# Tokens laid out by time up to the first experts, the recurrence in six chunks of 32 steps

## What is computed

```python
h = concat([patches @ proj_w.T + proj_b + pos_emb,                 # 64 tokens a sample
            segm_table[mask] + sinusoid + token_table[x_txt]])     # 128 tokens a sample
# block 0: a linear recurrence over time in 64 blocks of 3 channels
x = layernorm(h)
b, d, u = x @ W_biv + b_biv, sigmoid(x @ W_decay + b_decay), x @ W_in + b_in
s_t = d_t * rotate(s_{t-1}, axis * angle = b_t) + u_t              # t = 0..191
h = h + s
# block 0: experts, top two of eight, one hidden layer of 288, gelu
h = h + sum_k gate_k * expert_{top k}(layernorm(h))
# block 1: linear attention with 12 heads, then layernorm and experts (768 hidden, silu)
h = h + attention(layernorm(h));  h = h + experts2(layernorm(layernorm(h)))
```

## Time and profile before

| | |
|---|---|
| median of three runs | 540.99 us |
| profiled execution, its own time | 542.78 us |
| its span | 541.0 us |
| VectorE busy | 305.7 us, 57% of the span |
| TensorE busy | 373.5 us, 69% |
| ScalarE busy | 157.5 us, 29% |
| GpSimd busy | 210.9 us, 39% |
| mean clock granted to TensorE | 0.80 of full |

### The profile page before, as it was taken

One profiled execution on the slowest core, in us unless ns is written; L12 is line 12 of the kernel. 1 busy time (PEld: TensorE's weight loads), 2 busy tenths in 40 slices (PEclk: granted clock), 3 DMA queues, 4 the chain that ended last, 5 costly groups with the idle time before them and its releaser, 6 DMA issues.

```text
span 541.0 us, 8003 instructions
## 1 busy us (share of the span) xinstructions
PE 373.5 (69%) x2351; PEld 317.8 (59%) x2351; DVE 305.7 (57%) x1493; ACT 157.5 (29%) x315; POOL 210.9 (39%) x207
## 2 busy tenths in 40 slices
PE   5795002040272699999619989781599999999993
PEld 5442001030162488888508758681499999999992
DVE  4879999999858245445365236969333333333320
ACT  1299405120034011111025111444043333333320
POOL 4204696900002467776300000005445555465433
PEclk9698555555555599999859999765599999999998
DMA  9465000000010112222199900042112333333222
GB/s 250 43 168 121 1 1 1 1 30 1 0 59 1 51 59 81 73 81 76 38 294 312 269 2 0 0 138 67 57 32 50 54 51 52 53 53 53 43 23 22
DMA packets 35884, 37.29 MB, mean 69 GB/s; under 512 B 5898, under 2 KB 32190, under 8 KB 35842
## 3 DMA queue, kind: packets, MB, share of 16 engines
q1 hardware_dynamic: 24342, 21.28, 14.0%
q0 software_dynamic: 9312, 14.00, 12.9%
q10 hardware_dynamic: 2188, 1.49, 1.0%
HBM read 26.41 MB, written 10.35 MB: 68 GB/s over the span
## 4 chain that ended last, share of the span: by engine, by line
PE 34%; DVE 29%; DMA 24%; issue 7%; ACT 3%; POOL 1%; POOLq 1%; SPq 0%; DVEq 0%; ACTq 0%
DMA out<-reg,idxs 20%; DVE bank L992 8%; DVE reg L982 8%; PE bank L1497 7%; PE bank L1456 6%; PE bank L1601 3%; PE bank L1399 3%; PE bank L1483 2%; PE bank L1613 2%; PE bank L1538 2%; DVE st L886 2%; PE bank L1381 1%; DMA con<-in_consts 1%; PE bank L1442 1%; POOL reg L572 1%
## 5 line engine op out<-in xcount | busy, mean ns | idle before, releaser
L1497 PE MATMUL bank<-reg 128*128 (+1 forms) x558 | 105.7, 335 | 1.4 <-DVE reg L1172 0.7
L1497 PEld LDWEIGHTS bank<-reg 128*128 128x128 f32 (+1 forms) x558 | 90.1, 191 | 11.8 <-issue 7.8
L599 POOL DMA_INDIRECT out<-reg,idxs x31 | 49.0, 1582 | 63.3 <-DMA out<-reg,idxs 52.3
L583 POOL DMA_INDIRECT reg<-xn_rows,idxs x62 | 60.5, 977 | 30.2 <-issue 17.9
L1183 DVE TENSOR_SCALAR reg<-bank,gs 128x192 f32<-128x192 f32 x31 | 13.0, 418 | 96.5 <-PE bank L1497 96.5
L992 DVE TENSOR_REDUCE bank<-reg 128x6 f32<-128x24 f32 x384 | 53.3, 184 | 0.0
L982 DVE TENSOR_TENSOR reg<-reg,bank 128x24 f32<-128x24 f32 x384 | 51.7, 175 | 0.1
L1471 PE MATMUL bank<-xTs,xT 128*128 128x128 f32 x372 | 47.9, 280 | 0.0
L1471 PEld LDWEIGHTS bank<-xTs,xT 128*128 128x128 f32 x372 | 45.2, 196 | 0.0
L752 ACT ACTIVATE reg<-bank 128x384 f32<-128x384 f32 x31 | 15.2, 491 | 99.8 <-PE bank L1475 99.8
L1381 PE MATMUL bank<-con,xn 128*96 128x128 f32 x72 | 14.2, 358 | 37.3 <-ACT xn L653 37.3
(11 more groups left out here) (246 smaller groups left out, 756.1 us busy)
## 6 DMA issues: line engine op xcount, KB each, us to landing
reg<-in_w2b SPq DMA_DIRECT2D x8, 576.0 KB, 9.2
reg<-in_w1b SPq DMA_DIRECT2D x8, 384.0 KB, 9.3
reg<-in_w1a SPq DMA_DIRECT2D x8, 216.0 KB
reg<-in_w2a SPq DMA_DIRECT2D x8, 216.0 KB
xn_rows<-xn SPq DMA_DIRECT2D x4, 384.0 KB, 2.6
reg<-in_w1b SPq DMA_DIRECT2D x16, 96.0 KB, 7.9
xn<-expert_rows SPq DMA_DIRECT2D x3, 384.0 KB, 6.6
a<-expert_rows ACTq DMA_DIRECT2D x3, 384.0 KB, 8.0
```

The costliest lines, as they stand in the source:

```text
L583: pool.indirect_dma_start(xs[:, i % RING, 0:(D, D2)[l]], None, xd[l], bass.IndirectOffsetOnAxis(ap=idxs[:, i:i + 1], axis=0)).then_inc(xs_ ...
L599: pool.indirect_dma_start(out, bass.IndirectOffsetOnAxis(ap=idxs[:, i:i + 1], axis=0), ys[:, i % RING, :], None, compute_op=ALU.add).then_ ...
L1497: ins = MM(bank[6][:, 0:D], (hTs if l == 0 else hT2[:, p])[0:r, c * P:(c + 1) * P], w2v[0:r, bass.ds(e * (nhc * D) + c * D, D)], start=(c ...
```

## The change

The host now orders patches and text by time. Tile 2q+f of the first block holds 32 consecutive steps of four samples, with partition = 4 * time + sample; a pair of tiles is one chunk (chunks 0 and 1 are the patches, 2 to 5 the text). TCH is 32, there are six chunks, buffers of the matrix preparation exist twice. For each chunk:

- `bivectors(c)` and `inject(c)` replace `projections`: products with 64 output rows and 128 moving columns, 32 and 24 instructions (24 and 24 for chunk 0, its decay with 8 apart), written directly to the half of the partitions where the scan wants them.
- ScalarE's `front(c)`: sigmoid of the decay, squares directly from PSUM, one copy of the bivectors, one strided copy of the inputs into the matrices.
- `table_of(func)`: a one-column activation that loads the next table in advance.
- The states of chunk g, when ScalarE has copied them, are transposed back with `h` added in PSUM by TensorE (`back(g)`), and ScalarE copies the sum to `h` (`h_copy`). Norm start, norm end, transposes, logits and top two of chunk g lie at fixed step numbers of the next chunks.
- Text embeddings are added by GpSimd; text norms lie inside chunk 0's steps.
- The small constants come in an array `small` of their own, loaded first; `sinpos` and `bp` come in chunk layout (393 and 295 KB) into the region of the first experts' weights.
- The normalized rows are written to `xn_rows` in batch order, four DMAs a chunk, and `h` to `h_rows` likewise; after the last chunk `h` is loaded back in batch order, and the gates go through `gate_rows` and 16 DMAs. `xn_rows` and `expert_rows` have 2048 rows for each of the two choices, part of them padding, and index constants follow.

The diff at its core:

```diff
-TCH = 64
+TCH = 32
@@ matrices: two buffers of each, 128 columns
         def unit(n):
-            v = carve(reg1, n * U)
-            return v.rearrange("p (c a t) -> p c a t", c=n, a=NCH)
+            return [carve(reg1, n * U).rearrange("p (c u) -> p c u", c=n) for _ in range(2)]
@@ SyncE
-            for g in range(3):
-                js = slice(4 * g, 4 * g + 4)
-                sp.wait_ge(xn_ready, NJ + 4 * g + 4)
-                sp.dma_start(tok_rows(xd[0])[:, js, :], xn[:, js, :]).then_inc(xd_written, 16)
+            for g in range(NCHUNK):
+                sp.wait_ge(xn_ready, NJ + 2 * g + 2)
+                to_batch(sp, xd[0], xn, g, xd_written)
+                sp.wait_ge(h_copied, g + 1)
+                to_batch(sp, hd, h, g, h_stored)
+            sp.wait_ge(h_stored, 16 * NCH * NCHUNK)
+            by_batch(sp, h, hd, [h_loaded] * 3)
+            sp.wait_ge(gate0_ready, 1)
+            sp.dma_start(gd, gate[:, :, :].rearrange("p k j -> p (k j)")).then_inc(gate_stored, 16)
...
@@ GpSimd
+            for q in range(4):
+                pool.wait_ge(seg_ev, q + 1)
+                pool.wait_ge(gath[q], 32)
+                nc.gpsimd.tensor_tensor(h[:, js, :], h[:, js, :], xn[:, js, :], ALU.add).then_inc(emb_ready, 1)
...
-            for c in range(1, NCHUNK):
-                prep_angle(pool, nc.gpsimd, link, c)
-                prep_matrix(pool, nc.gpsimd, link, c)
+            # sum_squares, reduce_angle, prep_matrix of 1, the same of 2, then
+            sum_squares(3); reduce_angle(3); sum_squares(4); prep_matrix(3); reduce_angle(4); prep_matrix(4)
+            sum_squares(5); reduce_angle(5); prep_matrix(5)
@@ ScalarE
+            def front(c):
+                xb, yb = proj_banks(c)
...
+                act.wait_ge(proj_mm, 2 * c + 1)
+                if c:
+                    nc.scalar.activation(dec[:, c * U:(c + 1) * U], xb[:, 3 * U:4 * U], ACT.Sigmoid)
+                if c >= 2:
+                    act.wait_ge(th2_ready, c - 1)
+                xv = xb[:, 0:3 * U].rearrange("p (c u) -> p c u", c=3)
+                nc.scalar.activation(sq[c % 2], xv, ACT.Square).then_inc(sq_ready, 1)
+                if c:
+                    nc.scalar.activation(biv[:, :, c * U:(c + 1) * U], xv, ACT.Copy)
+                    injections(c)
+            # from chunk 1 on, every call takes its place in this order (table_of in brackets)
+            front(1) [sqrt] theta(1) [sin] trig(1) [sqrt] ln_std(1,2) ln_std(1,3) ln_norm(1,2)
+            xt_evac(2) ln_norm(1,3) [sigmoid] front(2) [sqrt] theta(2) ln_std(1,4) ln_std(1,5)
+            [sin] xt_evac(3) trig(2) ln_norm(1,4) ln_norm(1,5) keep_states(0) xt_evac(4) xt_evac(5)
+            h_copy(0) [sigmoid] front(3) front(4) [sqrt] theta(3) ln_std(2,0) [sin] trig(3)
+            ln_norm(2,0) [sqrt] theta(4) keep_states(1) xt_evac(6) h_copy(1) [sin] trig(4)
+            [sigmoid] front(5) [sqrt] ln_std(2,1) theta(5) ln_norm(2,1) keep_states(2) xt_evac(7)
+            h_copy(2) [sin] trig(5) [sqrt]
+            for g in range(2, NCHUNK - 1):
+                ln_std(2, g); ln_norm(2, g, h); xt_evac(NPAIR + g); keep_states(g + 1); h_copy(g + 1)
@@ VectorE
+            begin(0); recip_of(1); steps(0, 4); ln_text(2); ln_text(3); steps(4, 6); ln_end(1, 2)
+            ln_end(1, 3); steps(10, 4); ln_text(4); ln_text(5); steps(14, 10); recip_of(2)
+            steps(24, 4); ln_end(1, 4); ln_end(1, 5); steps(28, 4); begin(1); steps(32, 12)
+            ln2_start(0); steps(44, 14); recip_of(3); ln_end(2, 0); steps(58, 6); begin(2)
+            steps(64, 14); ln2_start(1); recip_of(4); steps(78, 4); topk(0); steps(82, 14); begin(3)
+            steps(96, 6); ln_end(2, 1); steps(102, 8); recip_of(5); ln2_start(2); steps(110, 8)
+            ln_end(2, 2); steps(118, 2); topk(1); steps(120, 8); begin(4); steps(128, 8); topk(2)
+            steps(136, 6); ln2_start(3); steps(142, 6); ln_end(2, 3); steps(148, 12); begin(5)
+            steps(160, 4); topk(3); steps(164, 10); ln2_start(4); steps(174, 6); ln_end(2, 4)
+            steps(180, 12); topk(4); ln2_start(5); ln_end(2, 5)   # norm of chunk 5 on VectorE
@@ TensorE
+            def half_mms(bk, col, c, cc, m0, hf):
+                for k in range(NK):
+                    r = rows(k)
+                    ins = MM(bk[64 * hf:64 * hf + 64, col:col + U], wst[0:r, k, cc, m0:m0 + 64],
+                             xT[0:r, k, (2 * c + hf) * P:(2 * c + hf + 1) * P], start=(k == 0), stop=(k == NK - 1))
+                return ins
+            def back(g):
+                pe.wait_ge(hist_copied, g + 1)
+                pe.wait_ge(xT_ready, NPAIR) if g == 0 else pe.wait_ge(h_copied, g)
+                for f in range(2):
+                    MM(bank[1][...], ident, h[:, 2 * g + f, :].rearrange("p (n c) -> p c n", c=3),
+                       start=(f == 0), stop=False)
+                for c in range(3):
+                    ins = MM(bank[1][...], histf[..., c], ident, start=False, stop=(c == 2))
+            ... t_pair(1, 2) bivectors(2) t_pair(1, 3) inject(2) bivectors(3) inject(3)
+            t_pair(1, 4) t_pair(1, 5) bivectors(4) inject(4) back(0) bivectors(5) inject(5)
+            t_pair(2, 0) logits(0, 0)
+            for g in range(1, NCHUNK):
+                back(g); t_pair(2, g); logits(0, g)
```

More of the change, by code:

```diff
@@ new lines, in _ @@
+            ln_std(1, 0)
+            ln_norm(1, 0, h)
+            ln_std(1, 1)
+            ln_norm(1, 1, h)
+            table_of(ACT.Sigmoid)
+            front(0)
+            theta_of(act, link, 0)
+            table_of(ACT.Sin)
+            xt_evac(1)
+            trig_of(act, link, 0)
+            injections(0)
+            table_of(ACT.Sigmoid)
+            front(1)
+            table_of(ACT.Sqrt)
+            theta_of(act, link, 1)
+            table_of(ACT.Sin)
+            trig_of(act, link, 1)
@@ new lines, in _ @@
+            dve.wait_ge(sq_ready, 1)
+            link(V.tensor_copy(biv[:, :, 0:U],
+                               proj_banks(0)[0][:, 0:3 * U].rearrange("p (c u) -> p c u", c=3)))
+            dve.sem_inc(biv_ev, 1)
+            text_rows(1)
+            reduce_angle(dve, V, link, 0)
+            recip_of(dve, V, link, 0)
+            text_rows(2)
+            text_rows(3)
+            dve.wait_ge(seg_ev, 4)
+            for b in range(2):
+                V.memset(ring[b][:, :, :, 3:4], 1.0)
@@ new lines, in ln2_start @@
+            def ln2_start(g):
+                dve.wait_ge(h_copied, g + 1)
+                ln_start(2, g, h)
+            begin(0)
+            recip_of(dve, V, link, 1)
+            steps(0, 4)
+            ln_text(2)
+            ln_text(3)
+            steps(4, 6)
+            ln_end(1, 2)
+            ln_end(1, 3)
+            steps(10, 4)
+            ln_text(4)
+            ln_text(5)
+            steps(14, 10)
+            recip_of(dve, V, link, 2)
+            steps(24, 4)
+            ln_end(1, 4)
@@ new lines, in _ @@
+            ln_end(1, 5)
+            steps(28, 4)
+            begin(1)
+            steps(32, 12)
+            ln2_start(0)
+            steps(44, 14)
+            recip_of(dve, V, link, 3)
+            ln_end(2, 0)
+            steps(58, 6)
+            begin(2)
+            steps(64, 14)
+            ln2_start(1)
+            recip_of(dve, V, link, 4)
+            steps(78, 4)
+            topk(0, 0, GROUPS[2][0])
+            steps(82, 14)
+            begin(3)
+            steps(96, 6)
+            ln_end(2, 1)
@@ new lines, in _ @@
+            steps(102, 8)
+            recip_of(dve, V, link, 5)
+            ln2_start(2)
+            steps(110, 8)
+            ln_end(2, 2)
+            steps(118, 2)
+            topk(0, 1, GROUPS[2][1])
+            steps(120, 8)
+            begin(4)
+            steps(128, 8)
+            topk(0, 2, GROUPS[2][2])
+            steps(136, 6)
+            ln2_start(3)
+            steps(142, 6)
+            ln_end(2, 3)
+            steps(148, 12)
+            begin(5)
+            steps(160, 4)
@@ L1563, in _ @@
+            inject(4)
+            back(0)
+            bivectors(5)
+            inject(5)
             t_pair(2, 0)
-            t_pair(2, 1)
             logits(0, 0)
-            pe.wait_ge(hist_copied, NGRP)
-            for ch in range(NCH):
-                for c in range(3):
-                    ins = nc.tensor.transpose(bank[2 + ch][:, c * P:(c + 1) * P], hist[:, NPATCH + 1:T + 1, ch, c],
-                                              ident)
-                ins.then_inc(back_mm, 1)
-            for q in range(2, NPAIR):
-                t_pair(2, q)
-                if q == 4:
-                    logits(0, 1)
@@ L1577, in _ @@
-            logits(0, 2)
+            for g in range(1, NCHUNK):
+                back(g)
+                t_pair(2, g)
+                logits(0, g)
             ranks(0)
```

707 lines of the change are left out of this document (397 added, 310 removed).

## The result

The changed kernel took 562.63 us (median of 4 runs, 560.62 to 565.05) beside 540.89 us (540.35 to 542.60) for the kernel before: ratio 1.0375, interval 1.0326 to 1.0423. It is slower, as forecast, but by 21.7 us and not by 4.1, and outside the range of 530 to 556.

The account below looks back on a forecast made before the run. VectorE's serial recurrence was taken to bound the kernel ahead of routing. Start -16.2, pieces +11.8, tail -11.1 and stalls +19.6 gave +4.1 us, so 546.9 profiled and 545 median, range 530 to 556.

Parts of the forecast that it names:

- Start: Before the recurrence's first step: smaller constants and chunks start step 0 at 35.7 instead of 51.88 us, -16.2; bounds 33 to 38.
- VectorE's own pieces: Inside the recurrence: reciprocals, norm starts, norm ends and top-twos between unchanged steps take 19.7 us instead of 7.9, +11.8.
- Tail: From the last step to routing: only one chunk of two tiles left, 10.1 us instead of 21.2, -11.1.
- Waits: VectorE stalls ahead of reciprocal 2 and norm starts of chunks 0, 1, 2: 3, 6, 4, 6.5; sum given as 19.6 us.
- I take 118 at 1.2 and 62 at 2.4 GHz: TensorE's projections: assumed ns per 64-wide, 128-column matmul at each clock; upper bound 220 and 110, lower 59.
- 64-wide matmuls as dear as 128-wide: Rival on TensorE's projections: 220 and 110 ns each, stalls 1 and 2 become 6 and 12, 554 us; chance 0.07.
- Cold all through: Rival: TensorE stays at 1.2 GHz, stall 2 grows to 12 and stall 1 to 5, 555.5 us; chance 0.10.
- Routing to the end 377 us as before: After routing's first subtraction: expert stages and attention keep their shapes, so this stretch stays 377 us.
- no drain at the table loads: ScalarE's table switches cost only the load, 1.28 us; the rival with 1.38 more each gave 561 us, chance 0.03.
- SP's queue, gates and row writes cost nothing: Added DMA issues and round trips on SP's queue are hidden by slack: eight issues a chunk, 3.6 us in 16 or more.
- the stalls all came: Against the rival that VectorE's four waits mostly do not come: under 12 us in all, 535 us; chance 0.30.
- the reordering did a great deal: Against the rival that cheaper start and tail are taken by added pieces and half the stalls: 538.3 to 543.7; chance 0.20.

## Why the prediction was wrong

The profiled run of the changed kernel came out 18.1 us above the 546.9 forecast for it (565.05). Of these 7.7 are the waits, 5.9 the way behind routing, 4.2 three terms of 1 to 2 us each, and 0.5 lies around the span. The 6.1 us of the misread price (below) taken off the median of 562.63 leave 556.5, the 5.9 taken off leave 556.7, both just outside the range's 556: it took the two together (an estimate). By the steps of the prediction:

- **Start** (forecast -16.2): -14.3. The first step came 1.9 late, within the bounds. In other traces of the same front reciprocal 1 stood at 36.3 to 41.0, by TensorE's clock in its first groups (32 products in 2.88 or in 5.44 us).
- **VectorE's own pieces** (19.7): 168.53-37.56-82.9-27.3 = 20.8, right within 1.1. The step of 0.432 held (0.430). The norm starts were cheaper than 0.93 (two stand from 39.20 to 40.79, 0.8 each), and the first two ends dearer (both from 43.33 to 45.10, 1.8 where 0.7 was forecast), so part of the match is luck.
- **Tail** (10.1): 11.3. Most of this miss is a slip of addition: the prediction's own terms sum to 10.8, and with the signals to 10.9 to 11.1. The copy of h took 0.68 instead of 0.5 and the norm 0.7 instead of 0.4; the logits took the 1.9 forecast and the transposes 0.75, less than forecast.
- **Waits** (19.6): 27.3. This is the step that failed, and in it above all one term: the price of a half-width product, "I take 118 at 1.2 and 62 at 2.4 GHz". Order decides that price. The 24 of L1560 in the earlier trace rows alternate between the halves one by one. The eight of L1648, which the prediction called "eight that do not alternate", do: the code issues two products into rows 0 to 63 and then two into rows 64 to 127, and pairs by twos measured the same as strict pairs. Its records start some 44 ns apart in the trace of the kernel before, beside 112 for the 128-wide ones of L1653. So both rows came from pairs, while the changed kernel issues all products of one half and then all of the other. There they take 213 and 110 ns, and 192 and 93 in the mean with those at the changes of half. With them in pairs the four waits are 3.11, 7.06, 3.96 and 7.03 beside the forecast 3, 6, 4 and 6.5. That is 6.1 of the 7.7 us, shown by undoing it.
- **The rival with the right cause**, "64-wide matmuls as dear as 128-wide", forecast waits of 6 and 12; they are 6.1 and 10.1, and its 220 and 110 ns are 213 and 110 inside a half. It got 0.07 because the row that seemed to refute it had been misread. "Cold all through" is not it: the clock was 0.79 from 49 to 90 us, and the 56 products of chunk 4 ran at the high one.
- **"Routing to the end 377 us as before"**: 383.0 in the profiled run. This was taken from one trace without bounds. The same kernel gave 375.1 another time; it is spread, of up to 8 us, and the range should have held it. The Trainium skill, TensorE: Matmul & The Clock Gate, "Part 1: The HAM clock gate (the "warmup" mystery)", says that the number of products that run cold differs from run to run of one kernel; the traces agree (first group of the second projection 8.64 and 6.07 us in two traces of one kernel).
- **Other sums that were off, without weight**: the four waits add to 19.5; the kernel before has 10 table loads ahead of routing, not 9; and by their own waits the rivals of the cold clock and of the dear product come to 12.1 and 13.1 us late, not 14.6 and 13.6.
- **What held**: no drain at the table loads (1.28, the next activation 0.01 behind); matrices never last; SP's queue, gates and row writes cost nothing, as routing to the first products took the same 17 us in both; the sign.
- **The rivals that fell**: the stalls all came; the reordering did a great deal (start -14.3, tail -9.9) and lost more (pieces +12.9, waits +27.3).

The sum after the fact: -14.3+12.9-9.9+27.3=+16.0 at routing (179.84-163.90=15.9), and +5.9 behind it.

For the price of a narrow product there is a rule: the Trainium skill, TensorE: Matmul & The Clock Gate, "Part 3: Packing small matmuls — row/col tiling", says that small products placed at different positions of the array, by rows or columns, run at once. The runs agree (two records start 7 ns apart and together take the 213 or 110 ns of one), with the condition that this change missed: near neighbours in the queue must go to different halves.

## What to carry to other kernels

Here a float32 matmul half as wide cost as much as a full one unless its near neighbours went to the other half of the array; count what follows what in the queue before taking a price from a row. When work is interleaved into a serial loop, the loop's in-order partners have to deliver it in time: cut each feed first (order of issue on the feeding engines), then move the places where the loop asks, since moving those alone only shifts the wait. And a stretch that a change leaves alone still has a spread, here 8 us of 380 by TensorE's clock: take it from more than one trace. A mean over a group of records can mix two prices: look at single starts before calling a price something in between.

## What the hardware showed beyond that

- Records of 64-column float32 products with 128 moving columns start 213 ns apart at the low clock and 110 at the high one within one half; alternating between the halves, by ones or by twos, two take that time together (115 to 117 and 59 to 60 ns apiece over a group, with its start and end). Where 16 or 12 of one half are followed by as many of the other, only eight around the change do so.
- In one kernel the granted clock in the same stretch was 0.66 in one trace and 0.89 in another, and a low stretch of 7 us within the attention came in one of them only.
- The kernel before took 541 to 543 us in three sets of runs and 558 in two others; the stretch behind routing was some 15 us longer there in every kernel. Between the first two traces of the kernel before, all 13.8 us lie in the first experts: from routing to the load of their results pass 106.0 us in the first and 119.8 in the second. The second's chain has four waits of 3.2 to 3.5 us there, which the profile gives to "another core or an unknown queue" and the first's chain doesn't have. What causes them is open.
